# Moving GpSimd's holds one group back and its pauses from every group to every second group, in a two-layer graph kernel

## The reference

```
h = relu(layernorm(x))
x = x + L0(h)      # msg = h[src] @ weight[edge_type]; summed over edges by dst
h = relu(layernorm(x))
x = x + L1(h)      # msg = relu([h[src], h[dst], edge_attr] @ W1 + b1) @ W2 + b2; summed by dst
```

## Time and profile before

| | |
|---|---|
| time, median of 3 runs | 4875.33 us (4866.49 to 4877.28) |
| time of the profiled execution | 4865.98 us |
| its span, first to last instruction | 4863.8 us |
| POOL busy | 3372.5 us (69%) |
| PE busy | 2742.2 us (56%) |
| DVE busy | 1465.5 us (30%) |
| ACT busy | 577.6 us (12%) |
| mean granted TensorE clock | 0.70 |

### The profile page before, as it was taken

How to read it: one execution, slowest core, us unless ns; L and a number is a source line. 1 busy time by engine, 2 the same in 40 slices (tenths; PEclk the granted TensorE clock), 3 DMA queues, 4 the chain that set the end, 5 groups by cost and what they waited for, 6 DMA issues and landing times.

```text
span 4863.8 us, 37713 instructions
## 1 busy us (share of the span) xinstructions
PE 2742.2 (56%) x10310; PEld 1539.6 (32%) x10310; DVE 1465.5 (30%) x2002; ACT 577.6 (12%) x1139; POOL 3372.5 (69%) x3742
## 2 busy tenths in 40 slices
PE   2655555556555555555565646555555555556555
PEld 1433333334333333333332222222222222222222
DVE  6322222222222222222232323332323332323333
ACT  3111111111111111111110001000000010000000
POOL 7576666667667666666757777777777767777776
PEclk9777777777777777777766666666666666666666
DMA  4111111111111111111111112111112112112111
GB/s 102 21 25 25 25 27 25 25 27 25 25 27 25 25 25 27 25 25 27 25 29 28 31 30 32 29 31 31 30 30 32 29 30 31 30 30 32 29 31 28
DMA packets 391187, 144.15 MB, mean 30 GB/s; under 512 B 321650, under 2 KB 337323, under 8 KB 391163
## 3 DMA queue, kind: packets, MB, share of 16 engines
q0 software_dynamic: 106304, 109.07, 11.7%
q1 hardware_dynamic: 282245, 34.18, 4.9%
q10 hardware_dynamic: 2614, 0.62, 0.1%
HBM read 129.03 MB, written 12.83 MB: 29 GB/s over the span
## 4 chain that ended last, share of the span: by engine, by line
POOL 52%; issue 31%; another core or an unknown queue 6%; PE 5%; DVE 3%; DMA 1%; SPq 1%; POOLq 1%; DVEq 0%; ACT 0%; ACTq 0%
POOL rows L710 48%; PE ps L1379 2%; POOL spacer L743 2%; POOL spacer L763 2%; PE ps L1386 1%; DMA rows<-h_table,idx 1%; PE ps L1462 1%; PE ps L1461 1%; DVE z_slot L1230 0%; DVE q_blk L1243 0%; DVE slots L1219 0%; POOLq L359 0%; PE ps L1466 0%; DVEq L1234 0%
## 5 line engine op out<-in xcount | busy, mean ns | idle before, releaser
L710 POOL DMA_INDIRECT rows<-p_table,idx x1661 | 1576.2, 949 | 702.9 <-issue 629.5
L710 POOL DMA_INDIRECT rows<-h_table,idx x1533 | 1448.2, 945 | 711.7 <-issue 514.9
L1379 PE MATMUL ps<-onehot,rows 128*64 128x256 f32 x3328 | 676.7, 568 | 619.3 <-DMA rows<-h_table,idx 518.8
L1461 PE MATMUL ps<-w_attr,attr_t 64*128 64x512 f32 x416 | 407.2, 1079 | 1001.6 <-DVE q_blk L1243 714.9
L1095 DVE TENSOR_TENSOR onehot<-key,ps 128x2048 f32<-128x2048 f32 x209 | 475.5, 2278 | 656.5 <-remote 428.5
L1379 PEld LDWEIGHTS ps<-onehot,rows 128*64 128x64 f32 x3328 | 354.2, 200 | 861.5 <-issue 792.9
L1219 DVE TENSOR_TENSOR slots<-ps,rows 128x512 f32<-128x512 f32 x208 | 143.9, 692 | 1427.1 <-DMA rows<-p_table,idx 881.8
L1386 PE MATMUL ps<-w_types,slots 128*128 128x128 f32 x3328 | 466.2, 295 | 95.6 <-issue 91.9
L1386 PEld LDWEIGHTS ps<-w_types,slots 128*128 128x128 f32 x3328 | 427.3, 207 | 171.2 <-issue 163.5
L1461 PEld LDWEIGHTS ps<-w_attr,attr_t 64*128 64x128 f32 x416 | 98.0, 292 | 1039.2 <-issue 1039.1
L1462 PE MATMUL ps<-q_blk,onehot 128*128 128x512 f32 x416 | 423.5, 1121 | 0.0
(11 more groups left out here) (142 smaller groups left out, 1874.2 us busy)
## 6 DMA issues: line engine op xcount, KB each, us to landing
rows<-p_table,idx POOLq DMA_INDIRECT x1661
rows<-h_table,idx POOLq DMA_INDIRECT x1533
attr<-in_edge_attr_dram SPq DMA_DIRECT2D x52, 128.0 KB
q_win<-q_table SPq DMA_DIRECT2D x208, 32.0 KB
p_table<-pq_out SPq DMA_DIRECT2D x25, 120.0 KB
q_table<-pq_out SPq DMA_DIRECT2D x25, 120.0 KB
out_dram<-xs SPq DMA_DIRECT2D x25, 120.0 KB
xs<-in_x_dram SPq DMA_DIRECT2D x6, 480.0 KB, 6.3
```

The source lines that it names most:

```text
L710: pool.indirect_dma_start(rows[:, u, t, :], None, table, bass.IndirectOffsetOnAxis(ap=at, axis=0)).then_inc(s, 16)
L1379: last = pe.matmul(slot_ps[t % 2 * D:(t % 2 + 1) * D, b, t // 2, :], rows[:, u, t, :], onehot[:, b, t, :], start=True, stop=True)
L1461: pe.matmul(pre_ps[:, u % 2, :], attr_t[half, u // 2, :], w_attr[half].rearrange("k j d -> k (j d)"), start=True, stop=False)
```

## The change

It does three things on POOL, in the loops of both layers. The hold is lowered by one group: group g is fetched once group g - 3 is summed (layer 0) or added (layer 1). The wait for `spaced` stands only ahead of even groups. The memset stands only behind odd groups, but there two of them, with a wait for the first between them. The number of memsets and of waits for them stays the same: two of each in two groups.

```
+            def space(n):
+                pool.memset(spacer[:], 0.0).then_inc(spaced, 1)
+                wait_apart(pool, spaced, n + 1)
+                pool.memset(spacer[:], 0.0).then_inc(spaced, 1)
...
                 def turn_of_rows(it, last=False):
                     for u in range(U):
-                        wait_apart(pool, spaced, (it - 2) * U + u + 1)
+                        if u % 2 == 0:
+                            wait_apart(pool, spaced, (it - 2) * U + u + 1)
...
-                        wait_apart(pool, slots_summed, 2 * AHEAD + 2 * (it * U + u - 1))
+                        wait_apart(pool, slots_summed, 2 * AHEAD + 2 * (it * U + u - 2))
                         for t in range(SKIP if last and u == U - 1 else 0, T):
                             gather(h_table, u, t, rows_in[u])
-                        pool.memset(spacer[:], 0.0).then_inc(spaced, 1)
+                        if u % 2 == 1:
+                            space((it - 2) * U + u)
```

More of the change, by code:

```diff
@@ L754, in turn_of_groups @@
                     for u in range(U):
-                        wait_apart(pool, spaced, (NIT - 2 + it) * U + u + 1)
+                        if u % 2 == 0:
+                            wait_apart(pool, spaced, (NIT - 2 + it) * U + u + 1)
                         if u == 0:
@@ L759, in turn_of_groups @@
                             wait_apart(pool, batch_in[u // B], 16 * (it + NIT - 1))
-                        wait_apart(pool, pre_added, it * U + u + AHEAD - 1)
+                        wait_apart(pool, pre_added, it * U + u + AHEAD - 2)
                         for j in range(SKIP if last and u == U - 1 else 0, T):
                             gather(p_table, u, j, rows_in[u])
-                        pool.memset(spacer[:], 0.0).then_inc(spaced, 1)
+                        if u % 2 == 1:
+                            space((NIT - 2 + it) * U + u)
                 with pool.Fori(0, NIT - 1) as it:
```

## The result

| | before | after |
|---|---|---|
| median of 4 runs each | 4870.96 us | 4948.79 us (4934.34 to 4968.22) |
| profiled execution | 4865.98 us | 4955.24 us |
| its span | 4863.8 us | 4953.0 us |
| POOL, PE, DVE busy | 3372.5, 2742.2, 1465.5 us | 3368.8, 2631.0, 1473.8 us |

The ratio is 1.0156, with a 95% interval of 1.0138 to 1.0175: slower by 78 us, where 89 us less was forecast. Two things happened: the pauses became shorter, as they should, and POOL lost more than that in its holds. From POOL's first gather to its last, the loop of layer 0 grew by 33 us and layer 1 by 49 us.

The account below looks back on a forecast made before the run. POOL, 52% of the chain that ended last, was taken to bound the kernel. Savings of 70.7 + 2.5 + 6 + 10 = 89 us off 4865.98 gave 4777, adjusted to 4782 us, 1.9% faster; range 4750 to 4900.

Parts of the forecast that it names:

- So the 70.7 us go: Layer 0's loop: with the hold one group back, late raises are met in time, saving the holds' 70.7 us.
- Layer 0's holds: POOL's 50 held starts in layer 0's loop, 118.7 us idle; their price of 70.7 us was to go.
- First hold: First hold of layer 0's loop (23.81 us): POOL would start at 214.9 in place of 217.38, saving 2.5 us.
- Layer 1's holds: DVE held POOL four times in layer 1, 10.7 us; less 4 x 0.96, some 6 us saved.
- The odd group's start: Gap ahead of odd groups: 0.96 us becomes 0.31, the satisfied wait and its raise hidden under the gather; upper end 0.90.
- The wait between the memsets: New wait between the pause's two memsets, both layers: 0.60 us taken, between 0.08 and 0.96.
- They bite in both layers: Rival: after sixteen gathers POOL must stop 0.7 us longer per pair in both layers, 140 us: 4922, slower; chance 0.14.
- Its point of decision: The both-layers rival decides the outcome from 89 / 200 = 0.45 us a pair on.
- The holds' time is only moved: Rival: PE's raises need the quiet time anyhow, POOL pays elsewhere, the 89 us return: 4871, no change; chance 0.07.
- Cheap wait between memsets: Rival: the wait between the pause's memsets costs as little as 0.08 us, 104 us less: 4678; chance 0.06.
- The extra raise costs between gathers: Rival: the helper's extra raise ahead of odd groups isn't hidden, 200 x 0.59 = 118 us: 4900, slower; chance 0.08.
- the signs named: Signs against the forecast included POOL idling over 0.96 us behind most second memsets, above all in layer 1; layer 1's groups averaging 11.1 to 11.2 us was expected.

Follow-up runs that it names:

- the two controls with PE: Kernel before with, per group of layer 1, four added matmuls of 128 columns (1.0146), or sixteen increments of a spare semaphore by PE's queue (1.0069).

## Why the prediction was wrong

**The step that failed** is "So the 70.7 us go". A late raise was taken as a fixed 13.5 us after a group's last gather, to be met by a group that starts 22.4 us after it. The runs show no such fixed delay. In the case of the earlier trace rows PE itself was late, behind the matmuls of a finished chunk: its row for that group's sum, which the prediction didn't look at, runs to 1547.53, so the raise at 1550.27 came 2.7 us behind PE, not 13.5.

```profile
1543.85 3.68 PE L1379 MATMUL ps<-onehot,rows 128*64 128x256 f32 x16
```

And in layer 0 the delay goes with the hold. From a group's last gather to ACT's copy of the second half of its sum, the median of the loop's 191 full groups is 7.5 us before, 8.8 with the pauses alone, 19.4 with the holds alone (17.7 when run again), 38.0 with the holds at g - 5, and 20.9 in the change, where it is over 22.4 us in 91 groups. A hold one group back lets PE fall about one more group behind, and then it bites again. Holds further back therefore save nothing (1.0055 and 1.0072 for one group, 1.0028 for three), and the shorter pauses, taken as near nothing in themselves, carry most of the loss (1.0144 alone).

**Term by term.** Layer 0's holds: -70.7 us forecast; "remote" and PE ahead of the gathers of the loop are 257.7 us less the first hold of 21.3, 236 us, in place of 118.7. First hold: 23.8 to 21.3 us, the 2.5 us as forecast. Layer 1's holds: -6 forecast (10.7 - 4 x 0.96 is 6.9), 10.7 us became 129.5. The odd group's start: 0.31 forecast, 0.30 to 0.31 measured, so the satisfied wait and its raise do go by under the gather. The wait between the memsets: 0.60 taken, 0.15 measured, near its lower bound of 0.08. So a pair changed by -0.5 us, not -0.05, and the new pause was 2.18 us, not 2.64; what that spared came back in held starts, and more.

**The rivals.** *They bite in both layers* (0.14, 4922 us) is what came about. Its point of decision, 0.45 us a pair on top of holds that have gone, was passed: by its own count the holds cost (189 + 79) / 200 = 1.34 us a pair (79 are the 70.7, 2.5 and 6 that were to go), where 0.7 was reckoned from the prologue's 3.3 us. Odd groups, held in the middle of a pair (41 of them, up to 8.48 us), were not in it. That its time is only 27 us off is luck: a second error goes the other way, the pauses gave 100 us, not 10. *The holds' time is only moved* is borne out in kind for the holds taken alone, which lost 0.6 to 0.7% more than it says. *Cheap wait between memsets* was near on its price (0.15 us, against 0.08) and wrong on its time. *The extra raise costs between gathers* did not happen. Of the signs named, the average group of layer 1 did grow (11.4 to 11.7 us), and POOL idled more than 0.97 us behind the second memset in 136 of the 199 pairs that have a gather behind them. It was held there in 85 of them, 71 in layer 0 and 14 in layer 1, so most of all in layer 0 and not, as the prediction had it, in layer 1.

**Raises and gathers.** More or fewer raises of PE changed nothing (1.0000, 0.9998, 0.9999); what wants space is POOL's gathers. The Trainium skill (VectorE: DVE Perf Modes, "The TRN2 errata") asks kernels with dense semaphore increments from several engines to space them, against a deadlock. No run here deadlocked, and these three don't bear out the increments as the cause. The Trainium skill (TensorE: Matmul & The Clock Gate, "The cost: per-tile semaphore tail") has 26.3 ns for an increment. The trace agrees in size where POOL is quiet, with 0.04 us from PE to DVE, and not under a row of gathers, where the same raise took 9.5 us.

**Shown and open.** Shown: while POOL issues gathers in a row, PE's results reach ACT, DVE and POOL late and one by one, and a pause lets out what has piled up; a pause of 1.29 us per eight or 2.18 per sixteen is too short, 2.85 per sixteen and 1.50 per eight are about equal, and 1.71 in layer 0 (by the timeline, 0.75 + 0.96) is a little better; in layer 0 PE falls as far behind as the hold allows; added matmuls of PE cost by their number, bare increments a tenth of that. Open: whether a long pause does more than short gaps of the same sum, since no run held the sum of before and divided it; and what PE lacks while POOL gathers. PE's records show its matmuls started long before their raises, but their ends are modelled, so late completions and late raises behind matmuls are not told apart. The holds alone lost their time in layer 0: its loop took 2274 us from first gather to last, where the two controls with PE of the same session, which leave layer 0 as it was, took 2255 and 2256; 8 us more passed ahead of layer 1. Why PE's further lag costs that much is not settled.

## What to carry to other kernels

An idle stretch on the bounding engine may be doing work for others: before shortening it, look in the trace at what the other engines receive in it. A delay read from a trace at a hold may be set by that hold: look at the producer's own rows, and expect the delay to grow when the hold is loosened. Test the two halves of a change apart, and count waits against a kernel of the same session. A hold that an engine waits out can be a pause that another engine needs anyway, so removing the wait need not be worth its length.

## What the runs showed of the hardware beyond that

- A memset that waits, by the helper, for the memset before starts 0.15 us after it; a gather behind such a wait and one more starts after 0.96 us, a gather behind a memset with no wait between after 0.17 us, a gather behind a gather after 0.30 us.
- One added matmul per group of layer 1 cost 0.09 to 0.10 us of the kernel's time whatever its width (1 or 128 columns), though PE is busy for little more than half of the span.
- The kernel before had medians of 4913, 4868, 4861, 4919 and 4921 us in five sessions; 4861 and 4921 come from a chip of the same number, so it isn't the chip alone. The spread is larger than most of the effects measured here.
